# Mixture of experts over fixed expert regions, routed in groups of four blocks, results scattered to their tokens

## What is computed

```python
    x = x + _L0_attn_a_ref(_layernorm(x, axis=-1), ...)
    x = x + _L0_ffn_ref(_layernorm(x, axis=-1), L0_ffn_gate_up_proj, L0_ffn_down_proj, L0_ffn_router_w)
    x = x + _L0_attn_b_ref(_layernorm(x, axis=-1), ...)
    x = x + _L0_ffn_ref(_layernorm(x, axis=-1), L0_ffn_gate_up_proj, L0_ffn_down_proj, L0_ffn_router_w)
...
        logits = h @ router_w.T
        probs = jax.nn.softmax(logits.astype(jnp.float32), axis=-1)
        vals, idx = lax.top_k(probs, TOP_K)
        if NORM_TOPK:
            vals = vals / vals.sum(axis=-1, keepdims=True)
...
            gate, up = jnp.split(h @ gup.T, 2, axis=-1)
            y = jax.nn.silu(gate) * up @ dp.T
            return (acc + cw[:, None].astype(acc.dtype) * y, None)
```

## Time and profile before

| | |
|---|---|
| three runs, median | 991.66 us (988.1 to 998.45) |
| the profiled execution, its own time | 980.89 us |
| its span in the profile | 979.1 us |
| mean granted clock of PE | 0.794 |
| recurrence, with the start | 0 to 252.6 |
| experts, turn 0 | 252.6 to 453.3 |
| attention | 453.3 to 764.3 |
| experts, turn 1 | 764.6 to 979.1 |

### The profile page before, as it was taken

One profiled execution on the slowest core, in us unless ns is written; L12 is line 12 of the kernel. 1 busy time (PEld: TensorE's weight loads), 2 busy tenths in 40 slices (PEclk: granted clock), 3 DMA queues, 4 the chain that ended last, 5 costly groups with the idle time before them and its releaser, 6 DMA issues. The chain is left out here.

```text
span 979.1 us, 13892 instructions
## 1 busy us (share of the span) xinstructions
PE 716.8 (73%) x4643; PEld 547.9 (56%) x4643; DVE 489.1 (50%) x1066; ACT 304.1 (31%) x574; POOL 278.7 (28%) x354
## 2 busy tenths in 40 slices
PE   2858889853695999812469999999997609599980
PEld 2646667742463766501347777777875506376660
DVE  6592979795151235445344656566563505122433
ACT  1422352410241434301013444444344003233430
POOL 0002010116124034176202333324245060502305
PEclk9877989856587999955557979789699558799995
DMA  6910000001532344221554405543300332324534
GB/s 213 318 46 1 1 0 1 1 0 65 130 101 94 108 124 133 84 75 48 65 66 66 59 15 61 66 53 39 42 3 2 82 106 64 126 87 129 165 122 129
DMA packets 63226, 75.65 MB, mean 77 GB/s; under 512 B 9411, under 2 KB 58187, under 8 KB 62551
## 3 DMA queue, kind: packets, MB, share of 16 engines
q1 hardware_dynamic: 57014, 57.98, 26.1%
q0 software_dynamic: 6144, 16.79, 5.5%
HBM read 33.43 MB, written 28.57 MB: 63 GB/s over the span
## 5 line engine op out<-in xcount | busy, mean ns | idle before, releaser
L1230 PE MATMUL bank<-f_wgu,f_xt 128*128 x368 | 139.4, 504 | 32.2 <-ACT f_xt L1285 24.1
L1324 DVE TENSOR_TENSOR f_hid<-f_act_g,bank 128x176 f32<-128x176 f32 x92 | 31.0, 337 | 192.7 <-ACT f_act_g L1292 166.7
L1230 PEld LDWEIGHTS bank<-f_wgu,f_xt 128*128 128x128 f32 x368 | 70.5, 204 | 70.7 <-issue 47.8
L1044 POOL DMA_INDIRECT back<-ys,f_slots x64 | 63.1, 986 | 153.5 <-DMA ys<-f_yout 120.7
L1252 PE MATMUL bank<-f_wd,f_hT 88*128 x368 | 98.7, 393 | 0.0
L1032 POOL DMA_INDIRECT xs<-xn,f_slots x64 | 63.2, 988 | 105.2 <-DVE f_slots L1001 65.6
L1623 POOL TENSOR_SCALAR_AFFINE_SELECT b_prob<-b_prob 128x512 f32<-128x512 f32 x60 | 38.4, 640 | 145.2 <-ACT b_prob L1911 145.1
L1911 ACT ACTIVATE b_prob<-bank 128x1024 f32<-128x1024 f32 x60 | 61.5, 1025 | 42.7 <-PE bank L1745 42.4
L1252 PEld LDWEIGHTS bank<-f_wd,f_hT 88*128 88x128 f32 x368 | 65.0, 197 | 6.2
L1985 DVE COPY_PREDICATED bank<-b_later,bank 128x512 f32<-128x512 int32 x60 | 41.5, 692 | 48.2 <-PE bank L1716 41.3
L1292 ACT ACTIVATE f_act_g<-bank 128x176 f32<-128x176 f32 x92 | 29.2, 318 | 107.2 <-PE bank L1230 84.2
(11 more groups left out here) (296 smaller groups left out, 1600.4 us busy)
## 6 DMA issues: line engine op xcount, KB each, us to landing
f_xin<-xs SPq DMA_DIRECT2D x92, 128.0 KB
ys<-f_yout SPq DMA_DIRECT2D x92, 128.0 KB
xs<-f_zero SPq DMA_DIRECT2D x2, 2944.0 KB, 21.8
b_QS<-b_qh SPq DMA_DIRECT2D x32, 128.0 KB, 4.6
b_KS<-b_kh SPq DMA_DIRECT2D x32, 128.0 KB, 6.1
f_wd<-in_wd SPq DMA_DIRECT2D x4, 968.0 KB
f_wgu<-in_wgu SPq DMA_DIRECT2D x2, 1408.0 KB, 8.4
x_tok<-in_x SPq DMA_DIRECT2D x4, 512.0 KB, 6.9
```

The source lines that it names most:

```text
L1044: pool.indirect_dma_start(back[:, n % GB, e], None, m.ys[h], bass.IndirectOffsetOnAxis(m.slots[:, h, e, i:i + 1], 0)).then_inc(m.got[n % G ...
L1230: mm = pe.matmul(psG[:, g % 2, 0:2 * FH], xt[:, g % 2, k * P:(k + 1) * P], m.gu[:, k, bass.ds(e, 2 * FH)], start=k == 0, stop=k == KD - 1)
```

## The change

Each expert gets a fixed region of 2048 rows in one DRAM tensor `xs` (16384 rows of 272 numbers). A row carries four more columns: the first choice's share, tanh of half the logit difference, the token number and the first choice's region. Unused rows hold zeros and a token number out of range. `xs` is filled once, by 8 DMAs (17.8 MB; before, 2 of 2944 KB).

Tokens are routed in four groups of four blocks, in 29 steps each. A running `next` per expert says where its next row goes, so a group can be scattered (8 indirect DMAs) as soon as it is routed. In turn 0, groups 0 to 2 are routed and scattered in passes 1 to 3 of the recurrence, in turn 1 in periods 9 to 19 of the attention. Group 3 is routed in `experts`; its scatters stand on POOL behind those of tiles 3 to 10. Part 0 of `Table` lists 17 tiles that groups 0 to 2 fill, part 1 the other 22 (39 tiles in place of 46). A tile's row and its expert's columns come from registers, on SP and on PE. Tile 17 is the first whose load waits for the scatters of group 3.

For each tile three DVE instructions of 128x1 (`aim`) find whether the rows are second choices, their share and their target. ACT's copy of y multiplies by the share, and POOL scatters the y rows to DRAM `back` at their token (`send_back`), where the store by SP was. There are no gathers. After the last tile SP brings `back` in (two DMAs of 512 KB for four blocks), DVE adds it to x in two instructions of 128x1024, and in turn 0 the norm, the transposes and the copies of four blocks follow. In turn 1 four stores of 512 KB follow all the loads. The tanh is made by ACT where exp was.

```diff
-                    if it == ROUTED_AT:
-                        pe.wait_ge(tl.xl_ready, now(it - 1))
-                        pe_logits(pe, m, xTh, xTl, 0, psY[:, 0])
+                    if it > 0:
+                        pe_ranks(pe, m, 0, it - 1, psB[:, 0])
...
                     project_out(it)
-                    if it == ROUTED_AT:
-                        pe_ranks(pe, m, 0, 0, psB[:, 0])
-                        pe.wait_ge(m.route, routed(0, 0, COPIED))
+                    if it > 0:
+                        pe.wait_ge(m.route, routed(0, it - 1, COPIED))
...
                     if it == NCH - 1:
-                        for i, c in pairs[:SENT_AHEAD]:
-                            pool_scatter(pool, m, xn, 0, 0, i, c)
+                        for i, c in SENDS[:SENT_AHEAD]:
+                            pool_scatter(pool, m, xn, 0, it - 1, i, c)
                     tail_pool(pool, tl, it)
-                for i, c in pairs[SENT_AHEAD:]:
-                    pool_scatter(pool, m, xn, 0, 0, i, c)
+                    if it > 0:
+                        for i, c in SENDS[SENT_AHEAD if it == NCH - 1 else 0:]:
+                            pool_scatter(pool, m, xn, 0, it - 1, i, c)
...
                     mean_squares(it)
                     if it == 0:
                         tail_split_dve(dve, t0, 3)
-                    if it == ROUTED_AT + 1:
-                        first.experts()
-                        first.slots()
-                        first.difference()
+                    else:
+                        group = Routing(dve, m, 0, it - 1)
+                        group.take(psY[:, 0])
+                        group.compare()
+                        group.choose()
                     if ahead:
                         decays(it + 1)
                         taps(it + 1, 0)
                     rms_split(it)
+                    if it > 0:
+                        group.take_counts(psB[:, 0])
+                        group.slots()
                     if ahead:
                         taps(it + 1, 1)
-                    if it == ROUTED_AT:
-                        first.take(psY[:, 0])
                     outputs(it)
-                    if it == ROUTED_AT:
-                        first.compare_equal()
-                        first.compare()
-                        first.choose()
+                    if it > 0:
+                        group.difference()
+                        group.payload(xn)
                     if ahead:
                         taps(it + 1, 2)
-                    if it == ROUTED_AT:
-                        first.take_counts(psB[:, 0])
-                    if ahead:
                         taps(it + 1, 3)
+                    else:
+                        group.shares(xn)
+                        table = Table(dve, m, 0, 0)
+                        table.tiles()
+                        table.experts()
+                        table.rows()
                     tail_stats_dve(dve, tl, it, add=True)
                     if ahead:
                         rotate(it + 1)
...
+XW = 272
...
+PART = (17, 22)
...
+TAKEN, RANKED, COPIED, SLOTS_KNOWN, DIFF_KNOWN, PAYLOAD, SHARED = 2, 10, 12, 22, 25, 28, 29
+TABLE_STEPS = (15, 18)
...
+        pool.wait_ge(m.filled, 16 * FILLS)
+        pool.wait_ge(m.route, routed(turn, g, SHARED))
+    pool.indirect_dma_start(m.xs, bass.IndirectOffsetOnAxis(m.slots[:, g, c, i:i + 1], 0), xn[:, g * TPC + i], None)\
+        .then_inc(m.sent, 16)
...
+                    sp.dma_start(xin[:, g % XB], m.xs[bass.ds(row, P)]).then_inc(x_in[g % XB], 16)
...
+                    for e in range(2):
+                        r0 = (2 * turn + e) * T + g * TPC * P
+                        sp.dma_start(back[:, g % 2, e], m.back[r0:r0 + TPC * P].rearrange("(b p) d -> p b d", p=P))\
+                          .then_inc(back_in[g % 2], 16)
...
+                for g in range(NGRP):
+                    bring(g)
                 if last:
-                    sp.wait_ge(stored, 16 * NU)
+                    for g in range(NGRP):
+                        sp.wait_ge(mix_done, 2 * (group_no(turn, g) + 1))
+                        sp.dma_start(out[g * TPC * P:(g + 1) * TPC * P].rearrange("(b p) d -> p b d", p=P),
...
+                def send_back(j):
+                    g = tiles(j)
+                    pool.wait_ge(y_done, g + 1)
+                    pool.wait_ge(aimed, 3 * (g + 1))
+                    pool.indirect_dma_start(m.back, bass.IndirectOffsetOnAxis(target[:, g % AR:g % AR + 1], 0),
+                                            yout[:, g % YB], None, bounds_check=2 * 2 * T - 1, oob_is_err=False).then_inc(y_out[g % YB], 16)
+
+                for j in range(G):
+                    send_back(j)
+                    if 0 <= j - SEND_AT < len(SENDS):
+                        pool_scatter(pool, m, xn, turn, g3, *SENDS[j - SEND_AT])
...
+                    act.wait_ge(aimed, 3 * g + 2)
...
+                    act.activation(yout[:, g % YB], psY[:, g % 2, 0:D], ACT.Copy, scale=share[:, g % AR:g % AR + 1])\
+                       .then_inc(y_done, 1)
...
+                    dve.tensor_scalar(second[:, r:r + 1], row[:, X_EXPERT:X_EXPERT + 1], m.region[:, j:j + 1], None,
+                                      ALU.not_equal).then_inc(aimed, 1)
+                    dve.wait_ge(aimed, 3 * g + 1)
+                    dve.scalar_tensor_tensor(share[:, r:r + 1], second[:, r:r + 1], row[:, X_TANH:X_TANH + 1],
+                                             row[:, X_SHARE:X_SHARE + 1], ALU.mult, ALU.add).then_inc(aimed, 1)
+                    dve.scalar_tensor_tensor(target[:, r:r + 1], second[:, r:r + 1], float(T),
+                                             row[:, X_TOKEN:X_TOKEN + 1], ALU.mult, ALU.add).then_inc(aimed, 1)
...
+                def mix(g):
+                    n = group_no(turn, g)
+                    dve.wait_ge(back_in[n % 2], 32 * (n // 2 + 1))
+                    for e in range(2):
+                        dve.wait_ge(mix_done, 2 * n + e)
+                        dve.tensor_tensor(xgrp(g), xgrp(g), back[:, g % 2, e].rearrange("p b d -> p (b d)"), ALU.add)\
+                           .then_inc(mix_done, 1)
...
+        LOGITS = {(9, 3): 0, (13, 3): 1, (16, 3): 2}
+        RANKS = {(10, 1): 0, (14, 1): 1, (17, 1): 2}
+        RATIOS = {(10, 4): 0, (14, 4): 1, (17, 3): 2}
+        SEND = {0: [(n, u) for n in (11, 12, 13, 14) for u in (0, 3)],
+                1: [(n, u) for n in (15, 16) for u in (0, 2, 3, 4)],
+                2: [(17, 4)] + [(n, u) for n in (18, 19) for u in range(NSTEP)][:7]}
...
+                        if (n, u) in LOGITS:
+                            g = LOGITS[n, u]
+                            pe.wait_ge(xl_done, TPC * (g + 1))
+                            if n // 2 + 1 < NHC and n % 2 == 1:
+                                pe.wait_ge(v_done, n // 2 + 2)
+                            else:
+                                pe.wait_ge(nmt_done, min(n, NB))
...
+                        if (n, u) in LOGITS:
+                            group = Routing(dve, m, 1, LOGITS[n, u])
+                            group.take(psJ[:, 2 * P:4 * P])
+                        if (n, u - 1) in LOGITS:
+                            group.compare()
+                            group.choose()
+                        if (n, u) in RANKS:
+                            group.take_counts(psJ[:, 3 * P:4 * P])
+                        if (n, u - 1) in RANKS:
+                            group.slots()
+                            group.difference()
+                            group.payload(xn)
+                        if (n, u) in RATIOS:
+                            group.shares(xn)
+                        if (n, u) == (18, 0):
+                            table = Table(dve, m, 1, 0)
+                            table.tiles()
+                            table.experts()
+                            table.rows()
```

600 lines of the change are left out of this document (313 added, 287 removed).

## The result

The changed kernel takes 949.38 us (median of 4 runs, 945.32 to 954.61) against 990.98 for the kernel before (988.1 to 998.45). The ratio is 0.9623, 95% interval 0.9575 to 0.967. The profiled execution took 952.93. Some executions run at a lower granted clock and take 1.5% and more longer, whatever the kernel, and the medians of experiments and their ratios leave these out.

What follows compares the result with a forecast made beforehand. No engine bounds it throughout: PE mostly fills tiles and attention, a DVE chain the recurrence, heads and tails are mostly empty. Terms sum to -48.2 on the profiled 980.9, giving 932.7, times 1.011 = 943 us; range 920 to 960.

Steps and rivals of the forecast that it cites:

- Recurrence, +25.8: Recurrence: routing in pass 1 adds 8.2, POOL's scatters ahead of rms and PE's clock lengthen passes 2 and 3; +25.8 us.
- The sign that I gave for pass 2, 50: Recurrence: expected trace sign, passes of 49, 50 and 50 us, with rms starting 6 late in passes 2 and 3.
- Tiles, -41.9 and -35.9: Tiles from the fifth, turns 0 and 1: 93.7 us each, without combines or the 16-scatter burst and its 16.3 us hole.
- Scatter of y and `aim`, nothing: Tiles: y scatter on POOL, 1.27 per tile, and aim's DVE steps, some 0.2 each, both hidden; no cost.
- every indirect DMA holds ACT: Rival, tile loop: each indirect DMA holds ACT 1.03 us, 97 us for 94; total 1040 us, chance 0.08.
- Head of turn 1, -30.5: First logits to fifth tile, turn 1: 26.5 us in place of 57.0, as groups 0 to 2 are already in DRAM.
- Tails, +5.4 and +3.6: Behind the last tile, turns 0 and 1: scatter, landing, loads and group work give 45.0 and 31.5 us.
- Attention, +24.3: Attention: logits, ranks and steps 13.8, scatters delaying masks 6.0, last group and table 3.5 + 1.0; +24.3 us.
- Fill, nothing: Filling xs with 17.8 MB takes some 79 us, done near 106, before the first scatter near 177; no cost.
- the ACT stall: Rival, tiles 3 to 10: dense POOL scatters bring the hole back, 16.3 us per turn; total 976 us, chance 0.20.
- The insertions: Rival: routing work added to recurrence and attention is mostly hidden, 50.1 us shrinking to 20; total 913 us, chance 0.20.
- The case slower than before: Whole kernel slower by over 1%, chiefly if each indirect DMA in the tile loop holds ACT; chance 0.09.

Runs made afterwards that it cites:

- e1: Changed kernel, but in the recurrence POOL sends a group's eight scatters behind the next pass's rms, not ahead of it; 920.3 us.
- e5: The changed kernel unaltered, run again in a later series; 931.8 us, 0.984 of the kernel before.
- e2: Changed kernel, but turn 1's 24 scatters of groups 0 to 2 stand at the start of the expert stage, not between the attention's masks; 959.2 us.
- e7: Changed kernel, but turn 1's three groups are routed in periods 16 to 19 of the attention, not 9 to 17; 934.0 us, 0.983 of the kernel before.
- all seven: Seven profiles of the changed kernel and variants that route between the attention's periods; steady stretch (seventh to twelfth rstd) 93.0 to 98.1 us.

## Why the prediction held, point by point

The forecast was 943, own range 920 to 960; the measured median is 949. The gain came where it was forecast, in the tiles and in turn 1's head. That the number came so near is partly luck, as the terms show:

- *Recurrence, +25.8.* Measured +28.0. The start and pass 0 got 1.4, pass 1 6.4 (47.2 against 40.8; I had 8.2), pass 2 got 9.8 (I had 9.1), the rest 10.4 (I had 8.5). The sign that I gave for pass 2, 50, doesn't fit its own term: 45.4 + 9.1 is 54.5, and 55.2 came. The queue ahead of `rms` was the larger part, as worked out; its `rms` ended 13.6 behind the mean squares, not 10.8, since the first scatter began 1.3 ahead of the mean squares (178.84 against 180.19), not 4.0, and two of the eight were long (1.23, 1.62). e1 prices it at 16.2, and I had 15.9 (6.0 and 2.0 of clock in pass 2, 7.9 in pass 3).
- *Tiles, -41.9 and -35.9.* Measured -37.9 and -31.7, because 8 us of the hole came back. In the later profiles (e5) the tiles were 89.8 and 90.7; my 4.0 for small waits was not needed. But there the kernel before has no hole either, so the term is -31.2 and -19.9. The 33.2 that I counted as the burst's cost (16.3 and 16.9) depends on a condition that I took for a property of the kernel. This is the step that failed on the later series: the ratio is 0.98 there and not 0.96. I also read the waits too narrowly: of the three in the earlier trace rows, 9.8 in all, one of 2.76 stands behind gathers, so the gathers did cause such a wait.
- *Scatter of y and `aim`, nothing.* Right. The period is 2.49 with 39 y scatters of 0.98. Of the waits that the rival "every indirect DMA holds ACT" needs, 49 us for 94 DMAs, ACT has 3.6 in turn 0 and 5.8 in turn 1, and none in e5.
- *Head of turn 1, -30.5.* -29.8; 26.5 was forecast, 27.2 came. The number holds, its contents partly by luck. The first product came 4.6 after the first logits (803.72 against 799.08), not 9, and the third came 11.2 behind the second because its rows waited behind the weights, where I had given the weights 1.
- *Tails, +5.4 and +3.6.* +3.1 and -1.0. In turn 0 scatter, landing and load took 9.3 (I had 10.3) and a group 7.18 (I had 8.2), together 5.1 less, and the last copies took 4.7, where I had 1.9. Turn 1's loads and stores took 26.9, where I had 31.5.
- *Attention, +24.3.* +39.6, and +29.4 to +41 in the later series. The term that is too small is the logits and steps, 4.6 a group: the steady stretch shows 14 for one and a half groups, some 9 a group. I priced them by their durations and left out that PE's clock may fall, which I had put into the recurrence's terms; it was 0.76 there in place of 0.83. The scatters' 6.0 is not seen in the middle (e2).
- *Fill, nothing.* Right: the first scatter goes out at 178.84 without a wait for it (its idle time ends with DVE's last step, L1029). The last of the eight fills was issued at 70.5 and none took over 22.2 to land, so they were done by 93, not 106.

The sum for the profiled execution was 932.7 and the profiled one took 952.9; the misses are the attention (15), the tiles (8) and the tails (-7). So 28 of the 48.2 were gained, and that is off by 20. That the median came nearer (949 against 943) is luck: the profiled execution of the kernel before had been its fastest, 10 below its median, and that of the changed kernel stood 4 above its own.

Of the rivals, the ACT stall came back at half its size in the first profile, 8 us in each turn, and not at all later. The insertions were not hidden: recurrence and attention got 67.6, where I had 50.1. The case slower than before was refuted by the tiles. The scatter of 1.50 in the earlier trace rows that I set beside a DVE copy ran beside another DVE instruction, `ol<-sq,oh` (230.37 to 232.13).

## What to carry to other kernels

When work is queued on an engine that also makes a small result on the critical path, look at what stands ahead of that result in the order. Eight scatters ahead of one `rms` cost 16 of this change's 28 us in the recurrence, and giving them the place behind it made the kernel 2% faster. Work put into a stretch where PE is nearly full can cost more than its own length: here 14 us for work that I estimate at 5, with PE's clock at 0.76 in place of 0.83. Price it from a stretch that has it, not from its instructions. And a loss that a single profile shows under some instruction should be seen in a second series of runs before its removal is counted as a gain.

## What the runs showed of the hardware

- The same kernel differed by 4% between series (991 against 950), with 33 us of it in two holes that the first series has and the three later ones, on three chips, don't. In the holes ACT waits up to 5.97 us at a time for something unnamed. In turn 0 these waits lie under or just behind rows of indirect DMAs on POOL, scatters and gathers, with and without table loads near. Such rows of DMAs are in all twelve later profiles too, without the waits. The cause is open.
- PE's granted clock was lower where the routing of turn 1 stood between the attention's periods: 0.83 in the steady stretch before and in e7, which has no routing there, 0.76 in e5 and 0.69 to 0.76 in all seven, at nearly the same count of matmuls. PE then seems fuller (82.94 of 93.0), but each matmul is longer.
- The Trainium skill's rule on the shared port ("SBUF — State Buffer", section "SBUF: two separate sides") would let DVE hold up scatters. Of the 71 indirect DMAs up to the end of turn 0's tiles in the profile after, one took 1.62 and one 1.23; all others took 0.96 to 1.11, some of them (181.63 to 184.15) beside DVE's `f_cmp` steps. So no run here shows that the port made the two long, and they are too rare to count.
